# A graph network on count matrices: 128-row transfers, and straight tiles stored as bytes by GpSimd's DMA

## The reference

```
L0:  3 times:  agg = segment_sum(h[src], dst);  z = (h + agg) @ W1 + b1;  z = relu(batchnorm(z)) @ W2 + b2
               (batchnorm and relu again, but for the last);  then rows divided by their length
L1:  agg = segment_sum(x[col], row) / degree;   relu(agg @ W1.T + b1) @ W2.T + b2
L2:  agg = segment_sum(x[src], dst) / degree;   relu(batchnorm(agg @ W_l.T + b_l + x @ W_r.T)) + x
L3:  w = edge_weight / sum of the weights into dst;  feat = relu(x @ W_pool + b_pool)
     neigh = segment_max(feat[src] * w, dst);  rst = x @ W1_self + neigh @ W1_neigh + b1;  h = relu(rst / |rst|)
     relu(h @ W2_self + segment_sum(h[src] * w, dst) / degree @ W2_neigh + b2)
after each:  x = layernorm(x + result)
```

## Time and profile before

| | us |
|---|---|
| median of 3 runs | 4169.85 (4158.0 to 4179.18) |
| profiled execution: its own time | 4173.97 |
| profiled execution: span of its trace | 4172.2 |
| from the start of tile 3's cast to that of tile 49's (46 tiles) | 1006.88 |
| eight blocks of dense pass 1 | 321.3 |
| eight blocks of dense pass 4 | 249.6 |
| granted PE clock, mean over the span | 0.91 |

### The profile page before, as it was taken

One profiled execution on the slowest core, in us unless ns is written; L12 is line 12 of the kernel. 1 busy time (PEld: TensorE's weight loads), 2 busy tenths in 40 slices (PEclk: granted clock), 3 DMA queues, 4 the chain that ended last, 5 costly groups with the idle time before them and its releaser, 6 DMA issues.

```text
span 4172.2 us, 59104 instructions
## 1 busy us (share of the span) xinstructions
PE 3334.2 (80%) x21633; PEld 2948.1 (71%) x21633; DVE 2545.4 (61%) x6179; ACT 2081.1 (50%) x3413; POOL 2073.6 (50%) x1795
## 2 busy tenths in 40 slices
PE   1577767776755888689979999997478989899998
PEld 0466656665654888589969988996367777777776
DVE  7899999999973533478872225445334444444446
ACT  0566666666655444467775545555233333333321
POOL 2233333233237767577777810000677777777740
PEclk9888988898887999899989989998689999999999
DMA  4356565656563455733323322331447767767765
GB/s 136 102 166 183 174 183 181 186 163 184 172 176 79 174 192 192 245 129 124 123 69 141 129 108 92 129 128 57 128 146 238 250 235 262 256 241 255 246 230 178
DMA packets 297382, 707.35 MB, mean 170 GB/s; under 512 B 82284, under 2 KB 157459, under 8 KB 281860
## 3 DMA queue, kind: packets, MB, share of 16 engines
q1 hardware_dynamic: 196346, 546.33, 36.7%
q0 software_dynamic: 85408, 97.26, 9.7%
q10 hardware_dynamic: 15338, 59.95, 4.4%
HBM read 499.35 MB, written 252.62 MB: 180 GB/s over the span
## 4 chain that ended last, share of the span: by engine, by line
PE 28%; POOL 20%; DVE 17%; DMA 16%; issue 12%; ACT 6%; ACTq 1%; SPq 0%; DVEq 0%; POOLq 0%
POOL PAN L419 19%; DMA PAN<-counts 10%; PE PS L637 9%; PE PS L544 7%; DMA PAN<-turned 4%; DVE XP L1057 4%; PE PS L527 2%; PE PS L546 2%; DVE XP L1059 2%; PE PS L1664 2%; DVE CX L482 2%; ACT CX L472 2%; DVE DEG L958 1%; DVE SSB L484 1%; DVE CP L482 1%
## 5 line engine op out<-in xcount | busy, mean ns | idle before, releaser
L419 POOL DMA_INDIRECT PAN<-table,src_i x832 | 819.1, 984 | 784.7 <-DMA table<-DEG 506.7
L900 POOL DMA_INDIRECT shares<-dst_f,spare x832 | 857.2, 1030 | 334.9 <-issue 252.1
L544 PE MATMUL PS<-XR,BB 125*125 125x385 bf16 x2500 | 642.0, 350 | 215.7 <-issue 206.1
L863 POOL CAST PAN<-BB 125x6250 uint8<-125x6250 bf16 x50 | 272.1, 5442 | 761.4 <-ACT BB L753 761.4
L544 PEld LDWEIGHTS PS<-XR,BB 125*125 125x125 bf16 x2500 | 363.9, 146 | 299.4 <-issue 216.5
L546 PE MATMUL PS<-ident_h,BB 125*125 125x125 bf16 x2500 | 568.1, 227 | 0.0
L637 PE MATMUL PS<-CX,XH 125*128 125x376 f32 x2000 | 473.7, 319 | 96.6 <-DVE CX L482 33.9
L1059 DVE TENSOR_SCALAR XP<-iota_h,ST 128x250 bf16<-128x250 bf16 x1250 | 509.1, 408 | 0.0
L764 ACT ACTIVATE PAN<-PS 125x625 uint8<-125x625 bf16 x500 | 347.3, 695 | 296.5 <-PE PS L546 287.0
L753 ACT ACTIVATE BB<-PS 125x1000 bf16<-125x1000 f32 (+1 forms) x350 | 425.2, 1215 | 136.7 <-PE PS L527 133.3
L1750 ACT ACTIVATE BB<-PAN,ew 128x128 f32<-128x128 f32 x832 | 254.1, 388 | 455.8 <-DMA PAN<-table,src_i 455.8
(11 more groups left out here) (324 smaller groups left out, 6524.6 us busy)
## 6 DMA issues: line engine op xcount, KB each, us to landing
PAN<-counts SPq DMA_DIRECT2D x300, 381.5 KB
shares<-SSB SPq DMA_DIRECT2D x70, 1600.0 KB, 21.7
XP<-shares SPq DMA_DIRECT2D x50, 1600.0 KB
PAN<-shares SPq DMA_DIRECT2D x50, 1600.0 KB
BB<-start_penalty SPq DMA_DIRECT2D x104, 512.0 KB
shares<-blank ACTq DMA_DIRECT2D x15, 3200.0 KB, 14.3
counts<-PAN SPq DMA_DIRECT2D x50, 762.9 KB
turned<-PAN POOLq DMA_DIRECT2D x50, 762.9 KB, 18.6
```

Of the source, the lines that this page charges most:

```text
L419: nc.gpsimd.indirect_dma_start(out=gbuf[g % 2][:, k, :], out_offset=None, in_=source, in_offset=bass.IndirectOffsetOnAxis(ap=src_i[:, t:t ...
L544: nc.tensor.matmul(agg_wide, count_tile[t % 2][:, j, :], x_wide[0:TN, j, :], start=(j == 0), stop=False)
L900: nc.gpsimd.indirect_dma_start(out=shares_flat, out_offset=bass.IndirectOffsetOnAxis(ap=share_at[:, t:t + 1], axis=0), in_=share[:, t:t + ...
```

## The change

It has three parts, and the diff below has all of it.

1. **128 rows.** The four tiles that are stored, and the panels that are loaded, are taken as 128 partitions instead of 125. The three added rows are filled with zeros once: SP issues five small DMAs for it, behind a new semaphore `rows_blank`, for which SP and POOL wait ahead of the first tile. What PE, ACT and DVE compute stays at 125 rows.
2. **The straight store.** POOL's cast and the byte tile go. POOL issues a DMA straight from the bfloat16 tile in BB to the bytes in `counts`, and the DMA converts. SP's store goes; SP's zero pieces wait for `hot_kept` (tile complete) instead of following the store. ACT, before it overwrites a tile two tiles later, waits for the DMA to have landed (`tile_out`) where it waited for the cast (`bytes_made`).
3. **Where the issues stand.** A new semaphore `bytes_turn` goes up by one on DVE behind bundle 2 and `keep_rows` of each tile from the second on; POOL's straight store of tile t waits for count t + 1. The two or three groups of share columns of a tile, which stood behind bundles 4 and 6 (and 1), stand together right behind that increment.

```diff
@@ buffers
-        count_tile = [w.rearrange("p (j d) -> p j d", d=TN) for w in
-                      (BB[0:TN, 0:TW].bitcast(BF16), BB[0:TN, 3200:3200 + TW].bitcast(BF16))]
-        bytes_of = [PAN[0:TN, 1600 * u:1600 * (u + 1)].bitcast(U8)[:, 0:N].rearrange("p (s f) -> p s f", s=NBLK)
+        tile_of = [BB[:, 3200 * u:3200 * u + TW].bitcast(BF16) for u in range(2)]
+        count_tile = [w[0:TN, :].rearrange("p (j d) -> p j d", d=TN) for w in tile_of]
+        whole_tile = [w.rearrange("p (s f) -> p s f", s=NSUB) for w in tile_of]
+        bytes_of = [PAN[:, 1600 * u:1600 * (u + 1)].bitcast(U8)[:, 0:N].rearrange("p (s f) -> p s f", s=NBLK)
@@ sp_cast_panels
-                    sp.dma_start(panel[u % NPAN][0:TN, :], turned[c, 0:TN, s * TW:(s + 1) * TW]
+                    sp.dma_start(panel[u % NPAN], turned[c, :, s * TW:(s + 1) * TW]
-                    sp.dma_start(panel[u % NPAN][0:TN, :], counts[c, s, 0:TN, :]).then_inc(panel_in[u % NPAN], 16)
+                    sp.dma_start(panel[u % NPAN], counts[c, s, :, :]).then_inc(panel_in[u % NPAN], 16)
@@ keep_bundle (ACT)
-                    act.wait_ge(bytes_made, t - 1)
+                    act.wait_ge(tile_out[t % 2], 16 * (t // 2))
@@ act_build_rest
-            act.wait_ge(bytes_made, NTILE)
+            for u in range(2):
+                act.wait_ge(tile_out[u], 16 * NTILE // 2)
@@ sp_build
+            sp.dma_start(PAN[TN:128, 0:3600].rearrange("p (m f) -> p m f", m=9), ...).then_inc(rows_blank, 16)
...
-            def store_tile(t):
-                sp.wait_ge(bytes_made, t + 1)
-                at = t % TPB * BLK
-                sp.dma_start(counts[t // TPB, :, 0:TN, at:at + BLK].rearrange("s p f -> p s f"),
-                             count_bytes[t % 2]).then_inc(tile_out[t % 2], 16)
+            sp.wait_ge(rows_blank, 80)
             for t in range(NTILE):
-                store_tile(t)
+                sp.wait_ge(hot_kept, NHOT * (t + 1))
@@ pool_build
-            def make_bytes(t):
+            def store_tile(t):
                 pool.wait_ge(hot_kept, NHOT * (t + 1))
-                if t > 1:
-                    pool.wait_ge(tile_out[t % 2], 16 * (t // 2))
-                nc.gpsimd.tensor_copy(count_bytes[t % 2].rearrange("p s f -> p (s f)"),
-                                      count_tile[t % 2].rearrange("p j d -> p (j d)")).then_inc(bytes_made, 1)
+                pool.wait_ge(bytes_turn, t + 1)
+                at = t % TPB * BLK
+                pool.dma_start(counts[t // TPB, :, :, at:at + BLK].rearrange("s p f -> p s f"), whole_tile[t % 2]
+                               ).then_inc(tile_out[t % 2], 16)
             def store_turned(t):
-                pool.dma_start(turned[:, 0:TN, t * BLK:(t + 1) * BLK].rearrange("s p f -> p s f"), stage[t % 2]
+                pool.dma_start(turned[:, :, t * BLK:(t + 1) * BLK].rearrange("s p f -> p s f"), stage[t % 2]
@@ dve_build
-                    if m in ((4, 6) if t % 4 else (1, 4, 6)) and 3 <= t < NTILE and shares_made[0] < T // GT:
-                        part(dve, shares_made[0])
-                        shares_made[0] += 1
+                    if m == 2 and 1 <= t <= NTILE:
+                        dve.sem_inc(bytes_turn, 1)
+                        for _ in range(2 if t % 4 else 3):
+                            if 3 <= t < NTILE and shares_made[0] < T // GT:
+                                part(dve, shares_made[0])
+                                shares_made[0] += 1
```

15 lines of the change are left out of this document (12 added, 3 removed).

## The result

| | before | after |
|---|---|---|
| median of 3 runs, us | 4169.85 (4158.0 to 4179.18) | 3822.91 (3820.78 to 3834.7) |
| profiled execution's own time, us | 4173.97 | 3820.78 |
| span of its trace, us | 4172.2 | 3819.0 |
| period of a tile, 46 tiles, us | 21.89 | 16.62 |
| eight blocks of pass 1, us | 321.3 | 276.85 |

The ratio is 0.9171, with a 95% interval of 0.913 to 0.9212: the changed kernel takes 8.3% less time. 3815 had been forecast.

What follows compares the result with a forecast made beforehand. DVE was taken to bound the build, five DMA engines pass 1, PE passes 2 to 4. Gains of 242 us (build) and 113 (128 rows), 355 in all, from 4173.97 gave 3819, stated as 3815; range 3740 to 3990.

Steps and rivals of the forecast that it cites:

- The cast: In the build, dropping POOL's cast gives DVE back 5.2 us a tile.
- The issues: In the build, POOL's two DMA issues a tile take 2.0 us each; 0.8 us was put for issues that start late.
- Share columns don't stand still: In the build, DVE's share columns go on while POOL issues its DMAs, so DVE loses nothing.
- The rival that had them stand still: In the build, share columns stop under issues or issues miss them: 2.4 us a tile, total 3900 us; chance 0.22.
- The conversion's price in the DMA engines: In the build, the converting store costs 79 engine-us a tile (57 to 114), all DMA together 229.
- The landing: In the build, the new store lands in 10 to 12 us; ACT's wait costs nothing unless landings pass 19 us.
- The period: Time per tile in the build falls from 21.9 to 17.0 us, gaining 225 us over 46 tiles.
- First tiles and the end of the build: The first tiles gain 12 us, and the build's end 5 us as the last cast leaves the chain.
- ACT's stand: ACT's stand of 24.60 us at a small DMA issue gets 4 us shorter (0 to 8).
- Pass 1: Eight blocks of pass 1 gain 71 us, since a block's DMA, 20.5 us, is less than PE's 31.2.
- Start of pass 2: The 29.35 us wait for a panel behind five zero slices shrinks by 20 us (0 to 29).
- Passes 2 to 4 and the rest: Pass 2's eight blocks gain 8 us; passes 3 and 4 gain nothing, since PE is full.

Runs made afterwards that it cites:

- e1: The changed kernel with share columns back behind bundles 4 and 6 (and 1) and without POOL's wait for `bytes_turn`; 3815.28 us, ratio 0.915.
- e6: The changed kernel with all 70 of SP's zero pieces of the build issued behind the last tile; 4090.19 us (single run), period 16.23 us.
- v5: The kernel of v4 unchanged, run again on another chip; 3791.21 us, ratio 0.9107 to the kernel before, period 15.60 us.
- e3: The changed kernel with panel loads back at 125 rows, stores left at 128; 3909.57 us, ratio 0.9378 to the kernel before.
- e7: The changed kernel with the ten zero slices of pass 1 moved to that pass's end, behind the five there; 3858.91 us, ratio 0.9272.
- e4: The changed kernel with panel loads and both stores at 125 rows; 4418.36 us, ratio 1.0633 to the kernel before, period 27.46 us.
- e9: The changed kernel with the converting store and the loads of `counts` at 125 rows; 5684.61 us (single run) where the kernel before takes 5525.43.
- e5: The kernel before, cast and SP's store kept, with all stores and loads at 128 rows; 4032.56 us, ratio 0.9672.
- e8: The changed kernel with a straight store that doesn't convert, so the stored bytes aren't the counts; 3799.8 us (single run), period 16.21 us.
- v3: The changed kernel with four stage buffers for turned tiles and zero slices in runs of 3200 bytes; 5194.35 us on the slow chip, ratio 0.9406.
- v4: v3 with share columns back behind bundles 4 and 6 and without POOL's wait; 5181.48 us on the same slow chip, ratio 0.9354.

## Why the prediction was right, step by step

*The cast* (5.2 us a tile off DVE). Right. DVE's busy time in the build fell by 6.0 us a tile, the 5.2 of the cast and 0.8 of the 1.2 that the issue had cost.

*The issues.* The price of 2.0 us each was wrong: 0.94 and 0.96 us were measured. It was carried over from 125-row transfers without asking whether the rows change it, though the same change alters them. With it falls the need for 4.3 us of cover, and the 0.8 us set aside for issues outside of it.

*Share columns don't stand still.* Right: 0.34 to 0.35 us under an issue. The rival that had them stand still is refuted; and it would have been worth some 0.5 us a tile and not 2.4, going by the one-hot rows of e1. The Trainium skill ("SBUF — State Buffer", "Who interferes with whom") has an instruction with two inputs in SBUF held up only by a GpSimd instruction that reads SBUF. The trace agrees if an issue doesn't read SBUF, which no row shows.

*The conversion's price in the DMA engines.* 79 engine-us a tile were taken, of 57 to 114; 91 were measured. With 58 for the turned store and 0.394 x 16 x 16.62 = 105 for the zeros (93 had been taken) the sum is 254, not 229, that is 15.9 us over 16 engines. The sum was too low by 1.6 us a tile, half of it by the conversion and half by the zeros, and the share came to 0.96, which the prediction had named as a sign of its own failure. It wasn't one: the share counts overlapping packets, and late zeros hold nobody up. Taking them out gave 0.4 us a tile (e6), where 0.5 had been put for queues.

*The landing.* 10 to 12 us expected, 13.5 measured, room until 19. Right in kind: ACT waits 13.3 us in all for the straight store. The turned store (15.8 us) was the one to watch: with four buffers for it, and no lining up, the period is 1.0 us shorter (v5).

*The period.* 17.0 forecast, 16.62 measured, 242 us for 225. DVE is busy 14.64 us of it (14.4 forecast) and idle 1.98. The forecast had 2.6 beside the work: 1.3 of idling, 0.8 for the issues, 0.5 for queues. The idling grew by 0.7, but nothing is to be seen of the other two terms.

*First tiles and the end of the build*: 12 and 5, with first blocks 10 and ACT's stand 4, 31 us in all; measured 7.7 + 22.7 = 30.4. ACT's stand went from 24.60 to 20.83 us, 3.8 as forecast, and with loads of 125 rows it is back at 24.37 (e3).

*Pass 1.* 71 us forecast, 44.4 measured. This term was mis-sized, by the largest margin of all. The sum of the DMA work of a block (20.5 us) was below PE's 31.2, and from that followed that PE would never wait. But the work isn't spread over the block: a slice comes as 128 runs of 25,600 bytes at once, and a panel behind it lands up to 14.0 us after its issue, while the four buffers hold only 12.5 us of PE's work. e7 and v5, which take the slices or their large packets away, read 31.4 and 31.6, the forecast; in v5 no panel takes over 8.4 us, and no engine waits for one.

*Start of pass 2.* 20 forecast, 4.7 measured; here the path was wrong. The wait of 29.35 us is indeed gone. The chain of the changed kernel now has at its place:

```profile
1380.07 12.96 DMA shares<-blank
...
1418.56 0.51 issue
1419.06 2.01 ACT CX L471 x5
...
1423.57 3.41 DVE CP L484
```

From 1418.6 to the stretch of pass 2 at 1499.9 casts and the splitting of x by DVE take turns, 81 us. Before, the way from the same casts (1737.4) to 1821.9 took 84 us, the wait with it; what came after the wait, from 1770.4, took 51. So some 30 us of that work had been done under the wait, and show now. What is late next was not asked here.

*Passes 2 to 4 and the rest.* 8 us forecast for pass 2, 9.6 measured; nothing for the others, and 10.3 + 2.5 + 8.8 = 21.6 measured. PE was busy 243.16 of 244.30 us in pass 3 and is 240.00 of 240.00 now; "PE is full" had been read off too quickly, but where the 3 us of it that were busy time, the shorter ways between the passes and the 8.8 us of the rest come from was not followed.

So 353 us came where 355 were forecast, but with misses of -27 (pass 1) and -15 (start of pass 2) against +17 (build) and +23 (pass 2 to the end) that cancel. The main mechanisms held (DVE freed of the cast, loads on 16 engines); how well the sum met was luck.

## What to carry to other kernels

If a tile is handed to the DMA engines, first see that its rows are a number that all of them can share: at 125 rows dropping a 5.4 us cast made this kernel 6% slower, at 128 rows 5% faster than with the cast. A type conversion in the DMA can take over a pass of a compute engine where most of the DMA work is such that nobody waits for it: here the store's packet time went from about 50 to 91 us a tile, and the time of the kernel by some 23 us. A DMA sum per block says nothing of a burst: behind a slice of large packets a panel took up to 14.0 us instead of 3.2. And when a wait goes, list what was done under it before its length is booked as a gain.

## What the runs showed of the hardware

- GpSimd's issue of a store of 10 runs a row takes 1.93 to 2.05 us for 125 rows (before, e4, e9) and mostly 0.94 to 0.98 us, at most 1.12, for 128, with conversion (the changed kernel) or without (e5, e8).
- A DMA by GpSimd that turns bfloat16 into bytes, 800,000 elements in 1280 runs, costs 91 us of packet time, 71 ns a packet of 625 bytes. Without conversion the same bytes cost 52 (e8, by GpSimd, in packets of up to 4375 bytes) and 49 (e5, by SP, in packets of 625).
- Of 125 rows, the converting store has some 2,800 packets of 4 bytes a tile besides and costs 133 to 142 us of packet time (e9, e4).
- Loads of 125 rows keep five packets in flight (84% of pass 4 before), loads of 128 rows up to 16 and more (16 or more for 22% of pass 4 after).
- A one-hot row (bfloat16, `tensor_scalar`) stood 5.4 us under a cast on POOL, to its end, but a pair of such rows took only 0.26 us longer under an issue of 1.0 us (e1).
- An issue of a slice on ACT takes 0.5 to 0.8 us while the queue takes it at once, and 8 to 13 us later in a row: the last six of fifteen slices of 128 runs (e7), the last three of five slices of 1024 runs (v5).
- One chip ran the kernel before in 5525 us. In the traces of v3, v4 and e9 from it the stretch ahead of pass 1, two blocks of pass 2 and the last stage are longer; the build and passes 1, 3 and 4 have the length that they have elsewhere.
